# Differential attention on one core: first sequence's output rows, norm and queries placed 0.4 to 0.5 unit earlier, and the first row maxima of the next attention spread over 4.7 units instead of 3.7

## What is computed

```
def _L1_attn_ref(x, W_attn, W_proj, ...):        # differential attention, 16 heads of 16 (keys: 8 + 8)
    qkv = x @ W_attn                              # q1, k1, q2, k2, v
    attn1 = einsum('bthd,bshd->bhts', q1, k1) * scale
    attn2 = einsum('bthd,bshd->bhts', q2, k2) * scale
    score = softmax(attn1 - lam * attn2, axis=-1)
    out = einsum('bhts,bshd->bthd', score, v)
    return ((1.0 - LAMBDA_INIT) * out.reshape(B, T, E)) @ W_proj

def _L1_xattn_ref(q, k, v):                       # context attention, 16 heads of 16, 1601 keys, masked
    scores = einsum('bqhd,bkhd->bhqk', qh, kh) / sqrt(16)
    scores = where(causal, scores, -10000.0)
    return einsum('bhqk,bkhd->bqhd', softmax(scores), vh)

x = x + _L1_attn_ref(_layernorm(x), ...)
x = x + _L1_xattn_ref(_layernorm(x), ctx, ctx)    # keys and values are the context itself
```

## Time and profile before

| | us |
|---|---|
| three runs | 1937.58, 1937.29, 1932.72 |
| median | 1937.29 |
| the profiled execution | 1937.35 |
| its span | 1935.6 |
| PE busy | 1754.9 (91%) |
| DVE busy | 1274.9 (66%) |
| ACT busy | 858.6 (44%) |
| POOL busy | 558.1 (29%) |
| mean granted TensorE clock | 0.951 of 2.4 GHz |

### The profile page before, as it was taken

How to read it: one execution, slowest core, us unless ns; L and a number is a source line. 1 busy time by engine, 2 the same in 40 slices (tenths; PEclk the granted TensorE clock), 3 DMA queues, 4 the chain that set the end, 5 groups by cost and what they waited for, 6 DMA issues and landing times.

```text
span 1935.6 us, 32748 instructions
## 1 busy us (share of the span) xinstructions
PE 1754.9 (91%) x12374; PEld 1137.1 (59%) x12374; DVE 1274.9 (66%) x2850; ACT 858.6 (44%) x1404; POOL 558.1 (29%) x945
## 2 busy tenths in 40 slices
PE   5999999999877899899899989997888899999988
PEld 4888888888765445455454445664554444444447
DVE  6767676675656777777778543444355688888844
ACT  3343433333342265645646732441232456666652
POOL 5543444443233140320501012441111223331230
PEclk9999999999988799999999979998897999999998
DMA  3000010110006457245264185644602157655100
GB/s 116 27 12 12 23 33 2 33 57 12 18 1 129 88 109 113 39 107 77 38 138 61 15 270 188 214 174 114 132 1 49 35 74 145 82 95 75 18 1 22
DMA packets 91480, 142.74 MB, mean 74 GB/s; under 512 B 14566, under 2 KB 59819, under 8 KB 91324
## 3 DMA queue, kind: packets, MB, share of 16 engines
q1 hardware_dynamic: 86924, 127.79, 31.3%
q10 hardware_dynamic: 2528, 7.74, 1.3%
q0 software_dynamic: 1872, 5.13, 0.7%
HBM read 109.68 MB, written 32.03 MB: 73 GB/s over the span
## 4 chain that ended last, share of the span: by engine, by line
PE 70%; DVE 16%; ACT 5%; issue 4%; POOL 3%; DMA 1%; SPq 0%; ACTq 0%; DVEq 0%; POOLq 0%
PE bank L1235 9%; PE bank L1195 9%; PE bank L1214 8%; PE bank L1956 5%; PE bank L1543 5%; PE bank L1842 3%; PE bank L777 3%; PE bank L1844 3%; PE bank L1843 3%; PE bank L1975 3%; DVE xa_part_max L1308 2%; PE bank L2418 2%; PE bank L2403 2%; PE bank L742 1%; DVE da_neg L2537 1%
## 5 line engine op out<-in xcount | busy, mean ns | idle before, releaser
L1308 DVE TENSOR_REDUCE xa_part_max<-bank 128x1 f32<-128x448 f32 (+1 forms) x512 | 269.9, 567 | 38.9 <-PE bank L1195 35.8
L1269 ACT ACTIVATE xa_e<-bank 128x1024 f32<-128x1024 f32 (+1 forms) x208 | 212.7, 1023 | 138.0 <-PE bank L1214 136.0
L1269 ACT ACTIVATE ca_e<-bank 128x1024 f32<-128x1024 f32 (+2 forms) x208 | 196.4, 957 | 89.1 <-PE bank L1214 88.3
L1308 DVE TENSOR_REDUCE shared<-bank 128x1 f32<-128x400 f32 (+1 forms) x384 | 206.7, 570 | 35.3 <-PE bank L1195 31.4
L1195 PE MATMUL bank<-xa_kst,xa_qst 122*128 122x448 bf16 (+1 forms) x512 | 164.6, 354 | 13.4 <-DVE xa_part_max L1308 8.7
L1235 PE MATMUL bank<-xa_e,xa_vaug 128*17 128x256 f32 (+2 forms) x1792 | 140.0, 387 | 1.6 <-ACT xa_e L1269 0.6
L981 POOL TENSOR_TENSOR gsa_qk<-gsa_qk,gsa_rot 128x512 f32<-128x512 f32 x64 | 81.9, 1280 | 164.7 <-DVE gsa_rot L897 164.7
L1235 PE MATMUL bank<-ca_e,ca_vaug 128*17 128x256 f32 (+2 forms) x1664 | 125.7, 375 | 3.2 <-POOL ca_e L1380 1.4
L1214 PE MATMUL bank<-xa_qst,xa_kst 128*128 128x256 bf16 (+1 forms) x832 | 127.3, 275 | 0.0
L1543 PE MATMUL bank<-xa_wkv,shared 128*128 128x256 f32 (+1 forms) x448 | 120.1, 397 | 7.6 <-SPq L281 3.4
L1195 PEld LDWEIGHTS bank<-xa_kst,xa_qst 122*128 122x128 bf16 x512 | 45.6, 98 | 109.0 <-DVE xa_part_max L1308 64.2
(11 more groups left out here) (402 smaller groups left out, 4223.9 us busy)
## 6 DMA issues: line engine op xcount, KB each, us to landing
xa_kst<-xa_k_parts SPq DMA_DIRECT2D x96, 200.1 KB, 8.1
ca_kst<-ca_k_parts SPq DMA_DIRECT2D x96, 200.1 KB, 8.1
xa_k_parts<-xa_parts SPq DMA_DIRECT2D x8, 1200.8 KB, 6.9
ca_k_parts<-moe_ctx_parts SPq DMA_DIRECT2D x8, 1200.8 KB, 5.7
moe_gu<-in_expert_gate_up SPq DMA_DIRECT2D x8, 1024.0 KB, 14.7
shared<-in_ctxT_split ACTq DMA_DIRECT2D x4, 1601.0 KB, 9.3
moe_ctxT<-in_ctxT SPq DMA_DIRECT2D x8, 800.5 KB, 8.4
ca_cv<-in_ctx SPq DMA_DIRECT2D x4, 1536.0 KB
```

What stands on the lines that cost most here:

```text
L1269: e.activation(self.e[m % 3][0:rows, :, first:T], banks[m % 2][0:rows].rearrange("p a (h t) -> p (a h) t", t=T)[:, :, first:T], ACT.Exp, s ...
L1308: e.tensor_reduce(top, work[:, 0:hi - lo], AX.X, ALU.max).then_inc(*reduced(t, *step))
```

## The change

Four numbers of places change, all for the first sequence (units 0 to 3) or for the context attention's first unit:

- the two `out_turn` steps and the two `out` steps of the first sequence: from 3.2 to 2.8 behind unit 3, that is from 6.2 to 5.8;
- its norm and queries: they begin at 3.8 instead of 4.3 behind unit 3, and are drawn together by a factor of 0.8, so that `ca_q` moves from 9.3 to 8.4;
- the load of the context attention's first queries: from 9.7 to 8.8;
- the 32 first maxima: they begin at 9.9 instead of 10.9 and still end at 14.6, that is 6.8 in a unit instead of 8.6.

No work is added or removed. The other sequences keep their places.

```diff
                 if n % UNITS == UNITS - 1 and n + 1 < N_DA:
-                    parts.append(added(n // UNITS, n + 3.2, 1))
+                    first_rows = n < UNITS
+                    parts.append(added(n // UNITS, n + (2.8 if first_rows else 3.2), 1))
                     if n + UNITS + 1 < N_DA:
-                        parts.append(queries_of(n // UNITS, n + 4.3, 1))
+                        parts.append(queries_of(n // UNITS, n + 3.8, 0.8) if first_rows else queries_of(n // UNITS, n + 4.3, 1))
             first = [("max", 0, h_, i, c) for h_ in range(UNIT) for i in range(TB) for c in range(len(ca_chunks))]
-            parts.append([(9.7, ("load", 0)), *spread(first, 10.9, 14.6), (14.6, ("neg", 0)), (14.6, ("neg_parts", 0)), (14.7, ("load", 1)), (15.3, ("neg_turn", 0))])
+            parts.append([(8.8, ("load", 0)), *spread(first, 9.9, 14.6), (14.6, ("neg", 0)), (14.6, ("neg_parts", 0)), (14.7, ("load", 1)), (15.3, ("neg_turn", 0))])
```

## The result

The change makes the kernel slower: the ratio to the kernel before is **1.0048, with an interval of 1.0030 to 1.0067**. The medians of 14 runs each are 1950.61 us (1939.32 to 1963.91) and 1939.83 us (1930.54 to 1951.50); their quotient alone is 1.0056, inside the interval. The executions of one kernel lie up to 25 us apart here, and their mean granted clock goes with their time: the change's slowest run has 0.941 of full speed, its fastest 0.955.

A forecast was written before the change was run, and what follows sets the result against it. PE bounds the kernel, busy for 91% of the span. A later top 12,0 (+1.6) and maxima (+2.8 - 3.5) give +0.9 us on 1937.35: 1938.2 us, own range 1935 to 1942, 8 in 10 within 1930 to 1947.

The forecast's parts named there:

- rival 2: Clock falls early, at 1437 to 1446, and stays low, 3.8 us a unit, some 9 us: 1947, chance 0.20.
- Turns and products sooner: First sequence's turns and products, around exp 7: PE waits of 2.4 us become 1.9, about 0.8 us won.
- Norm sooner: Turns of h ahead of exp 8: PE newly waits 2.0 us for POOL, costing 0.9.
- Queries sooner: Split of the queries ahead of da_qn: PE waits 1.6 us, before 0.95; top 11,1 about level.
- Load: Ahead of the first maximum: PE newly waits 1.4 us for the load; top 12,0 comes 1.6 us later.
- Maxima: Seven more maxima ahead of exp 11, seven fewer behind it: 2.8 us paid, 3.5 us taken back.
- Sum at full clock: Whole stage: +1.6 + 2.8 - 3.5 = +0.9 us, giving 1938.2 us.
- my case, with the low stretch much as it was: Main case: the low clock from exp 12 to exp 14 stays; 1938.2 us, range 1935 to 1942, chance 0.50.

The follow-up runs named there:

- e4: The change with the turns of h behind pv 7 and load and first maxima as in the kernel before; 0.9967 of the kernel before.
- e1: The change with load and first maxima put back as in the kernel before, rows and norm still sooner; 1.0022 of the kernel before.
- e2: The change with the two turns of h and ca_q moved behind pv 7; 0.9996 of the kernel before.
- e10: The change in its own order, with 52 unread matmuls in PE's waits from unit 8 on; 0.9959 of the kernel before.
- e12: e4 with unread matmuls in PE's waits from unit 8 on; 0.9957 of the kernel before.
- e8: e4 with 18 unread matmuls at six small PE waits of units 11 to 13; 0.9951 of the kernel before.
- e11: The kernel before with unread matmuls in PE's waits from unit 8 on; 0.9969 of the kernel before without them.
- e9: The change measured again, no edit; 1.0041 of the kernel before.
- e13: e4 measured again, unaltered, in a later group of runs; 0.9985 of the kernel before.
- e3: The change with nine unread matmuls in PE's wait for POOL ahead of the first turn of h; 1.0029 of the kernel before.
- e6: e2 with thirteen unread matmuls in PE's wait for the load ahead of the first maximum; 1.0001 of the kernel before.
- e5: e2 with the first maxima beginning at 10.4 instead of 9.9; 1.0001 of the kernel before.

## Why the prediction was wrong

The forecast was no measurable change, 1938.2 us; measured was slower by 0.48%, which on the 1937.29 us shown is 1946.6, and the median itself, in its own measurement, was 1950.61, above the range. What came is rival 2, priced at 1947 with a chance of 0.20. The steps one by one:

- **Turns and products sooner: 0.8 us won.** Right in sign, too small. From `exp 5` to `exp 8` e4's profile takes 18.2 us (6.82 + 5.65 + 5.69) where the one of before takes 19.8: 1.6 won. The waits that are left are near what I had walked, 1.03 and 0.62 us; but before there were two more than I counted, 0.45 us ahead of `top 8,1` and 0.32 ahead of the second half of the products. That is the place where the change is good.
- **Norm sooner: a new wait of 2.0 us for POOL.** Right: 2.38 and 2.37 us in the two profiles of the change, 2.35 in e1.
- **Queries sooner: 1.6 us ahead of `top 10,1`.** Right: 1.57 and 1.53.
- **Load: a second new wait of 1.4 us.** The wait is not there in the profiles of the change, since PE was later than I had it; with PE in time, e2 shows 3.17 us. The chain from POOL's end to the first maximum was 7.9 us there where I had 7.5. In e10, which has the change's order at full clock, POOL ends at 1444.35 and PE comes to this place at 1450.49: by those 7.9 us it would wait 1.8, an estimate, which is near my 1.4. Its thirteen products keep it to 1453.50, 1.2 us longer than needed.
- **Maxima: 2.8 us paid for seven, 3.5 taken back.** Too dear in the emptier unit. The windows from `exp 10` can't be compared as they are, because in e12 `exp 10` runs beside `top 11,1`. From the end of `exp 10` to `exp 11`, at full clock and with the same fills, e10 takes 10.73 us with seven maxima and e12 9.66 with one: 1.1 us for six, 0.2 each, which is my lower bound. Taken back in units 11, 12 and 14 are 2.2 us (26.5 against 28.8), and in unit 13, where e12's clock was 0.85, 0.6 against e8's 10.16. With 0.2 for the maximum ahead of `exp 10`, spreading the maxima is itself worth some 1.5 us at full clock, where I had 0.7. (15.81 less 4.3, halved, is also 5.8 and not 5.6; that changes the price of a maximum by 0.02.)
- **Sum at full clock: +0.9 us.** Not contradicted: e10 against e11 is -0.0010, which their intervals don't separate from zero or from +0.9. The profiles are finer. From `exp 3` to `exp 15` e10 takes 103.0 us and e11 103.6; with units 10 and 13 of e11 at the lengths that e12 and e8 have at 1.00 (11.63 and 10.16), e11 would take 101.0. That leaves e10 2 us above, or 0.8 without the 1.2 that its thirteen products take too long. Turns late as in e12 would be better, 99.8 us.
- **The clock: "my case, with the low stretch much as it was".** This is the step that failed. I had named the mechanism, two waits within 9 us at 1437 to 1446, and put against it that the early fall of the trace of before was over at once. What the runs showed in its place: in e9 the clock falls right behind the wait for POOL, already ahead of the second wait, and is at 0.50 for units 8 and 9 and most of 10, without a break from 1436.4 to 1466.5 us. With the clock held in the same order (e10) the loss is gone, 0.9959 against 1.0041. The unit behind that wait ran at 0.62, 0.50 and 0.82 in the three profiles that have the wait unfilled, and at 0.98 to 1.00 in all others, before's included.
- **Rival 2's price, 3.8 us a unit.** Near, but its sum is right in part by luck. Against the profile of before, e9 loses 11.3 us in units 8 to 11 and gets 8.7 back in units 12 and 13, whose low stretch rival 2 had kept. And for it I said that PE was busy for 90% of that stretch; by rows 2 it is 87% (25.83 of 29.8 us). The cost of the clock alone: e9 and e10 have the same order; units 8 to 14 differ by 11.7 us. By its clocks e9 spent some 40 us of them at 1.2 GHz (each window's length times twice what its clock lacks to 1). That is 0.29 us lost for each us at the low clock; I had 7.6 in 29.8, 0.26. The Trainium skill's rule of one half (TensorE: Matmul & The Clock Gate, Terms) would make it 20 us, an estimate. The traces show less. In part of that time PE waits for DVE at either clock (for `da_neg`, 1.11 us in unit 11 and 1.06 in unit 12 of the kernel before), and e10 spends 3.0 us on fills ahead of the first maximum, where e9 is late enough to need no wait.

The fall itself differs from run to run of one kernel. e4's profile has the unit from `exp 10` at 1.00 and 11.2 us, that of e13, the same kernel, at 0.65 and 14.8. In the first profile of the change the clock was at 0.52 in unit 6 already, ahead of the wait for POOL. So a cause can be shown here only in what a change of PE's idle time does to the ratio over many runs. e10 against e9 (0.0082), with e11 against the kernel before (0.0031) as the control, does that: what costs in the change is the clock, and it is PE's idle time that lets it fall.

**Open.** How much of the loss each new wait brings: the square says about 0.005 for the turns and 0.003 for the maxima (0.004 and 0.001 with e13), but e3 and e6, which fill one wait each, did not give these back. Whether early maxima cost anything by themselves: e2, e5 and e6 lie at 0.9996 to 1.0001, e4 and e13 at 0.9967 and 0.9985, though spreading the maxima is worth some 1.5 us at full clock. The clock of unit 10 was low, 0.50 to 0.63, in all five profiles with early maxima and no fill right ahead of them, and in two of five with the maxima as before (e8 and e13, 0.66 and 0.65). But in four of the five it had fallen before the first maximum: in the change, e9 and e3 in unit 9 or sooner, in e5 as shown above. Only in e2 does it fall there, behind the wait for the load. So a cause in the maxima themselves is not shown.

## What to carry to other kernels

Where PE is the bound but waits often for less than a microsecond, an order of the work must be judged by where it puts PE's idle time, not only by how much: this order has two new waits of 2.4 and 1.6 us near each other and was 9 us slower, and with its waits filled it was 8 us faster than the kernel before. Before tuning such an order by its times, put unread matmuls into the waits and measure both orders with the clock held; if the difference goes away, as it did here, tune the clock first and the order after. One wait filled by itself gave nothing that could be measured here (e3, e6). And moving a step sooner needs a look at the slowest engine in its chain: here POOL's 4.3 us for a root of two columns, which nobody had waited for until then.

## What the runs showed of the hardware

- Matmuls of 128 x 128 that nobody reads made the kernel faster: 0.0082 in the change (e10 against e9, 52 of them), and 0.0028 in e4's order (e12 against e13, in the same rounds). With eighteen of them e8 came out at 0.9951, against 0.9967 and 0.9985 of the same order without them; these intervals overlap. Four of them take 1.06 us of what was idle time.
- The clock did not come back for many microseconds of nearly unbroken work: in unit 9 of e9 PE was busy for 10.94 of 11.10 us at 0.50, and it stayed low for most of the next unit. These were the same matmuls that ran at 1.00 in other executions. The Trainium skill (TensorE: Matmul & The Clock Gate, A second HAM failure mode) tells of a kernel whose small idle times between groups of matmuls make the clock swing; the traces here agree: unit 12, with waits of 0.5 to 1.1 us, ran at 0.50 to 0.90 in the ten profiles that leave them idle, and at 1.00 in the four that fill them.
